# Moving the normalisation of token rows to GpSimd, and splitting a selection matrix, in a fused token, attention and expert kernel

## The reference, cut to what matters

```
# token layer: 8 steps along the sequence, up and down, width 64
a = einsum('bdl,od->blo', x, W1) + b1
for _ in range(8):
    up   = relu(a + shift_r(up) @ W2.T + b2)
    down = relu(a + shift_l(down) @ W2.T + b2)
h = relu(x*W3 + b3 + (shift_r(up) @ W4.T + b4) + (shift_l(down) @ W4.T + b4))
# attention layer, on the first norm of h: (h - mean) / sqrt(var + eps) over the 64 of a row
Q, K, V = norm(h) @ Wq.T, norm(h) @ Wk.T, norm(h) @ Wv.T
score[q, k, g] = relu(sum_d w_mlp[d] * relu(Q[q, g, d] - K[k, g, d]) + b_mlp)
h = h + softmax_k(score) @ V
# expert layer, on the second norm: 8 experts, the best 2 of each token
h = h + sum_e weight[e] * (gelu(norm(h) @ We1 + be1) @ We2 + be2)
```

## Time and profile before

| | us |
|---|---|
| median of 3 runs | 290.73 |
| the three runs | 289.77, 290.73, 297.43 |
| the profiled execution | 290.83 |
| its span in the trace | 288.6 |
| around the span | 2.23 |

### The profile page before, as it was taken

How to read it: one execution, slowest core, us unless ns; L and a number is a source line. 1 busy time by engine, 2 the same in 40 slices (tenths; PEclk the granted TensorE clock), 3 DMA queues, 4 the chain that set the end, 5 groups by cost and what they waited for, 6 DMA issues and landing times.

```text
span 288.6 us, 8043 instructions
## 1 busy us (share of the span) xinstructions
PE 267.2 (93%) x2954; PEld 97.8 (34%) x2954; DVE 243.2 (84%) x977; ACT 254.7 (88%) x646; POOL 41.3 (14%) x43
## 2 busy tenths in 40 slices
PE   8988999999999869899898999999988999999995
PEld 2444232333333223222233322333332223225463
DVE  2256999999999899999898999999989995783741
ACT  4345999999999999999999999999999999858462
POOL 3301100010000200104301110081110100041410
PEclk9999999999999999999999999999999999999999
DMA  6400000000000000050000000600000051002000
GB/s 157 143 0 2 5 2 2 0 3 2 2 1 2 1 2 2 1 141 10 0 2 1 2 2 9 159 2 0 2 1 3 2 134 34 1 0 76 8 16 20
DMA packets 5318, 6.90 MB, mean 24 GB/s; under 512 B 1632, under 2 KB 3272, under 8 KB 5280
## 3 DMA queue, kind: packets, MB, share of 16 engines
q1 hardware_dynamic: 5280, 6.40, 8.7%
HBM read 5.81 MB, written 0.58 MB: 22 GB/s over the span
## 4 chain that ended last, share of the span: by engine, by line
ACT 60%; PE 28%; DVE 7%; issue 3%; POOL 0%; DVEq 0%; ACTq 0%
ACT relu_ring L489 45%; PE bank L1203 7%; PE bank L946 6%; ACT hid L520 5%; PE bank L1083 5%; ACT sc_sb L498 4%; PE bank L988 3%; PE bank L952 3%; DVE relu_ring L640 1%; ACT state L458 1%; ACT L520 1%; PE bank L982 1%; ACT L498 1%; DVE sc_sb L655 1%; PE bank L1123 1%
## 5 line engine op out<-in xcount | busy, mean ns | idle before, releaser
L489 ACT ACTIVATE relu_ring<-bank,q_sb 128x256 f32<-128x256 f32 x421 | 163.1, 610 | 0.1
L640 DVE TENSOR_SCALAR relu_ring<-nk_sb,q_sb 128x256 f32<-128x256 f32 x568 | 155.5, 344 | 1.1 <-ACT nk_sb L474 1.0
L1083 PE MATMUL bank<-relu_ring,wsc 128*32 128x512 f32 x1024 | 127.1, 598 | 2.3 <-ACT relu_ring L489 1.1
L520 ACT ACTIVATE hid<-bank,b 128x512 f32<-128x512 f32 (+1 forms) x80 | 45.7, 644 | 9.8 <-PE bank L1203 9.7
L1083 PEld LDWEIGHTS bank<-relu_ring,wsc 128*32 128x32 f32 x1024 | 26.9, 109 | 57.5 <-issue 37.2
L1203 PE MATMUL bank<-xf,wf_sb 64*128 64x512 f32 (+1 forms) x160 | 40.4, 551 | 1.8 <-ACT hid L520 1.8
L946 PE MATMUL bank<-hid,wd 128*32 128x512 f32 (+1 forms) x320 | 31.6, 512 | 0.8 <-DVE prod L840 0.7
L393 POOL TENSOR_TENSOR rstd<-rstd,neg_half 128x4 f32<-128x4 f32 (+1 forms) x9 | 8.7, 966 | 108.1 <-DVE rstd L595 108.1
L1203 PEld LDWEIGHTS bank<-xf,wf_sb 64*128 64x128 f32 x160 | 14.6, 185 | 25.0 <-ACT hid L520 18.5
L840 DVE SCALAR_TENSOR_TENSOR prod<-bank,b,wbc 128x512 f32<-128x512 f32 (+1 forms) x20 | 12.8, 640 | 11.7 <-PE bank L946 8.5
L988 PE MATMUL bank<-state,tokw_sb 64*64 64x256 f32 x224 | 19.1, 407 | 2.9 <-DVE state L576 2.2
(11 more groups left out here) (104 smaller groups left out, 209.3 us busy)
## 6 DMA issues: line engine op xcount, KB each, us to landing
wbc<-gates SPq DMA_DIRECT2D x6, 512.0 KB, 5.8
wf_sb<-in_wf SPq DMA_DIRECT2D x1, 516.0 KB, 5.2
wd<-in_wd SPq DMA_DIRECT2D x1, 512.0 KB, 5.5
wbc<-gates SPq DMA_DIRECT2D x2, 256.0 KB, 4.1
out<-o_sb SPq DMA_DIRECT2D x3, 128.0 KB, 6.2
sel_f<-in_sel SPq DMA_DIRECT2D x1, 245.2 KB, 2.9
x_sb<-in_xw SPq DMA_DIRECT2D x1, 192.0 KB, 3.8
wa_sb<-in_wa SPq DMA_DIRECT2D x1, 192.0 KB, 3.4
```

The lines of the kernel that those rows point to most:

```text
L489: ins = nc.scalar.activation(relu_ring[:, n % RING, j, qi, :], keys, ACT.Relu, bias=q_sb[:, p, q:q + 1], scale=scale)
L520: nc.scalar.activation(hid[:, n % 8, 0:t], up_psum(k, i), ACT.Gelu, bias=b1[:, col:col + 1]).then_inc(gelu_ready, 1)
L640: ins = vec.tensor_scalar(relu_ring[:, n % RING, j, qi, :], nk_sb[:, p, :], q_sb[:, p, q:q + 1], 0.0, ALU.add, ALU.max)
L1083: ins = mm(bank[SCORE[blk % 2]][32 * j:32 * j + 32, :], wsc[:, s, :], relu_ring[:, n % RING, j].rearrange("p q k -> p (q k)"), start=(s == ...
```

## The change

DVE gives the normalised rows of the first norm of pairs 1 to 3, and of the second norm of units 0 to 2, to POOL: 24 tensor_scalar instructions, 12 of 128 x 64 and 12 of 128 x 128. POOL makes them right after its own power. DVE keeps pair 0's first norm and the second norms of units 3 and 4.

At the start, the selection matrix comes in two DMAs and is cast in two parts. The first three parts (which pair 0's inputs need) come first, on all 96 partitions; the last three are loaded and cast on 32 partitions only. PE stacks pair 0's inputs first and spreads the weights behind them; DVE instead of ACT casts them into `ws`. PE multiplies 7 blocks of zeros before, and 2 after, where there were 8 and 3. The two halves of `stack_inputs` have slots of their own.

All tables are new. `ACT_TILES` gives ACT 457 tiles instead of 456. Of the tables the diff below shows the two lines that the prediction speaks of.

```diff
     dict(
-        pe_stack=(-47,), pe_step=(-41, -39, -38, -36, -36, -35, -35, -34), pe_out=(-33,), pe_xa=(-24,),
+        pe_stack=(-44, -44), pe_step=(-42, -39, -38, -36, -36, -36, -33, -33), pe_out=(-31,), pe_xa=(-24,),
...
-WARM_UP, WARM_STACK, WARM_STEP, WARM_SLOTS = 8, 3, 1, 24
+WARM_UP, WARM_STACK, WARM_STEP, WARM_SLOTS = 7, 2, 1, 24
...
-        dve_top=(51,), dve_gates=(54,), dve_prod=(63, 66, 69, 71), dve_out=(78,), pool_norm=(55,),
-        pool_exp=(59,), pool_sum=(71, 71, 71, 74), dve_norm=(48,), dve_rec=(47,), dve_divide=(47,),
+        dve_neg=(36,), dve_pt=(38, 40, 41, 42), act_weigh=(46,), dve_resid=(47,), dve_xf=(50,),
+        dve_top=(51,), dve_gates=(55,), dve_prod=(63, 66, 69, 73), dve_out=(79,), pool_norm=(56,),
...
-            sp.dma_start(sel_f[:], sel_d).then_inc(ld_sel, 16)
+            sp.dma_start(sel_f[:, 0:3 * KX], sel_d[:, 0:3 * KX]).then_inc(ld_sel, 16)
+            sp.dma_start(sel_f[0:32, 3 * KX:], sel_d[0:32, 3 * KX:]).then_inc(ld_selw, 16)
...
             def norm1(p):
                 pool.wait_ge(h1_stats, p + 1)
                 inv_std(0).then_inc(rstd1_ready, 1)
+                if p >= 1:
+                    pool.wait_ge(rstd1_ready, p + 1)
+                    pool.wait_ge(xa_mm, p)
+                    for i in range(TT):
+                        ins = vec.tensor_scalar(xn1[:, i % 2, i // 2, :], h1[:, p, i, :], mv[:, 0, i, 0:1],
+                                                rstd[:, 0, i:i + 1], ALU.subtract, ALU.mult)
+                    ins.then_inc(xn1_ready, 1)
...
             def norm2(k):
                 pool.wait_ge(h2_stats, k + 1)
                 inv_std(1, UNITS[k]).then_inc(rstd2_ready, 1)
+                if k < len(UNITS) - 2:
+                    u = UNITS[k]
+                    pool.wait_ge(rstd2_ready, k + 1)
+                    if k >= 1:
+                        pool.wait_ge(xf_mm, k)
+                    for i in u.tiles:
+                        ins = vec.tensor_scalar(xn2[:, i], h2[:, u.pair % 2, i:i + 1, :].broadcast_to([P, 2, D]),
+                                                mv[:, 1, i, 0:1], rstd[:, 1, i:i + 1], ALU.subtract, ALU.mult)
+                    ins.then_inc(xn2_ready, 1)
...
             act.wait_ge(ld_sel, 16)
-            nc.scalar.copy(sel[:].rearrange("k s n -> k (s n)"), sel_f[:]).then_inc(sel_ready, 1)
-            act.wait_ge(ws_mm, 1)
-            nc.scalar.copy(ws[:, 0:D], bank[tokb(0)[1]][0:KX, 0:D]).then_inc(ws_ready, 1)
-            nc.scalar.copy(ws[0:64, D:2 * D], bank[tokb(0)[1]][0:64, D:2 * D]).then_inc(ws_ready, 1)
+            nc.scalar.copy(sel[:, 0:3, :].rearrange("k s n -> k (s n)"), sel_f[:, 0:3 * KX]).then_inc(sel_ready, 1)
+            act.wait_ge(ld_selw, 16)
+            nc.scalar.copy(sel[0:32, 3:6, :].rearrange("k s n -> k (s n)"),
+                           sel_f[0:32, 3 * KX:]).then_inc(sel_ready, 1)
...
+            dve.wait_ge(ws_mm, 1)
+            vec.tensor_copy(ws[:, 0:D], bank[tokb(0)[1]][0:KX, 0:D]).then_inc(ws_ready, 1)
+            vec.tensor_copy(ws[0:64, D:2 * D], bank[tokb(0)[1]][0:64, D:2 * D]).then_inc(ws_ready, 1)
...
+                if p == 0 and b == 1:
+                    pe.wait_ge(sel_ready, 2)
+                    for j in range(3):
+                        ins = mm(bank[tokb(0)[1]][0:KX, 0:WX], sel[0:KR, 3 + j, :], x_pc[0:KR, j, 0, 0:WX],
+                                 start=(j == 0), stop=(j == 2))
+                    ins.then_inc(ws_mm, 1)
                     keep_warm(WARM_STACK)
```

More of the change, by code:

```diff
@@ new lines @@
+    dict(
+        pe_stack=(-69, -65), pe_step=(-60, -58, -56, -55, -52, -50, -48, -45), pe_out=(-42,), pe_xa=(-34,),
+        pe_project=(-32,), act_stack=(-61,), act_step=(-60, -58, -57, -51, -50, -48, -45, -42),
+        act_out=(-41,), act_qk=(-24,), dve_step=(-60, -59, -58, -54, -53, -50, -47, -45), dve_stats=(-41,),
+        dve_xa=(-35,), dve_v=(-30,), pool_norm=(-44,), pe_values=(-31,), pe_keys=(2,), dve_mom=(-43,),
+        dve_aggr=(-43,)),
+    dict(
+        pe_stack=(-74, -74), pe_step=(-72, -70, -65, -64, -61, -57, -56, -54), act_stack=(-72,),
+        act_step=(-71, -66, -65, -63, -61, -58, -57, -55),
+        dve_step=(-72, -68, -66, -62, -61, -58, -56, -54), pe_out=(-52,), act_out=(-53,), dve_stats=(-52,),
+        pool_norm=(-59,), pe_xa=(-50,), dve_xa=(-49,), pe_project=(-47,), act_qk=(-48,), pe_values=(-46,),
+        dve_v=(-46,), pe_keys=(1,), dve_mom=(-52,), dve_aggr=(-52,))]
@@ L115 @@
[L115 removed]
+        dve_top=(50,), dve_gates=(50,), dve_prod=(58, 63, 65, 71), dve_out=(72,), pool_norm=(44,),
+        pool_exp=(45,), pool_sum=(47, 52, 59, 59), dve_rec=(45,), dve_divide=(45,), dve_mom=(45,),
+        dve_aggr=(45,), dve_stats=(45,), dve_lg=(49,), dve_gap=(50,), dve_num=(50,), dve_hot=(50,),
+        dve_den=(50,), dve_gw0=(50,), dve_gw1=(50,), dve_ohw=(50,)),
     dict(
[L117 removed]
@@ L962, in stack_inputs @@
                         pe.wait_ge(v_ready, FREED[p])
-                for b in range(2):
-                    if p >= 1 and b == 1:
-                        pe.wait_ge(xs_mm, 2 * p + 1)
-                    c = 1 + 2 * p + b
-                    rows = slice(32 * (c % 3), 32 * (c % 3) + KR)
-                    for i in range(3):
-                        ins = mm(stack_psum(p, b), sel[rows, i, :], x_pc[rows, i, c // 3, :],
-                                 start=(i == 0), stop=(i == 2))
-                    ins.then_inc(xs_mm, 1)
-                if p == 0:
+                else:
+                    pe.wait_ge(xs_mm, 2 * p + 1)
+                c = 1 + 2 * p + b
+                rows = slice(32 * (c % 3), 32 * (c % 3) + KR)
+                for i in range(3):
+                    ins = mm(stack_psum(p, b), sel[rows, i, :], x_pc[rows, i, c // 3, :],
+                             start=(i == 0), stop=(i == 2))
+                ins.then_inc(xs_mm, 1)
+                if p == 0 and b == 1:
[4 more added lines that the diff above has]
+                    ins.then_inc(ws_mm, 1)
                     keep_warm(WARM_STACK)
@@ L1246, in _ @@
             pe.wait_ge(sel_ready, 1)
-            pe.wait_ge(xpc0_ready, 1)
-            for j in range(3):
-                ins = mm(bank[tokb(0)[1]][0:KX, 0:WX], sel[0:KR, 3 + j, :], x_pc[0:KR, j, 0, 0:WX],
-                         start=(j == 0), stop=(j == 2))
-            ins.then_inc(ws_mm, 1)
             for n in range(FIRST, LAST):
@@ L1272, in _ @@
                 for p in range(PAIRS):
-                    for _ in due(n, p, TOKEN_AT[p], "pe_stack"):
-                        stack_inputs(p)
+                    for b in due(n, p, TOKEN_AT[p], "pe_stack"):
+                        stack_inputs(p, b)
                     for t in due(n, p, TOKEN_AT[p], "pe_step"):
```

116 lines of the change are left out of this document (50 added, 66 removed), and 8 rows, old and new, of the table ACT_TILES.

## The result

| | before | changed |
|---|---|---|
| median of 4 runs each, us | 290.55 | 294.07 |
| all runs, us | 289.77, 290.36, 290.73, 297.43 | 293.84, 294.07, 294.08, 294.5 |
| the profiled execution, us | 290.83 | 293.84 |
| its span, us | 288.6 | 292.1 |

The ratio of the changed kernel to the one before is 1.0132, with an interval of [1.0107, 1.0158]: slower by some 3.8 us. The ratio goes by the undisturbed runs, so the 297.43 us before is left out of it. The forecast was 291.3 us, with a range of 287.5 to 295.5, and "within 2%" as the likeliest class. Both held. The sum was 2.5 us too low against the profiled execution, and this chapter is about where those came from.

What follows compares the result with a forecast made beforehand. The prediction took the kernel as a 27.6 us start, then ACT's list, then a full PE stretch. +2.4 - 0.7 - 0.7 + 0 - 0.5 = +0.5 us on 290.83 gave 291.3 us, range 287.5 to 295.5.

Steps and rivals of the forecast that it cites:

- the 33rd gelu: Sign at unit 2's first gelu, 225.7 us before: to come 0.5 to 1.5 us later.
- Bound: From first tile to unit 2's gelus, ACT's list sets the time: busy 197.79 of 198.10 us.
- ACT's list, +2.4: Up to unit 2's first gelu: four more tiles, 1.6 us, and pair 1's two `last` instructions, 0.8 us.
- Relief of DVE, -0.7: In the slots, less DVE work lets ACT lose two hidden waits: -0.7 us, bounds 0 and -3.
- DVE sets the pace as well: Rival, chance 0.10: DVE's lists decide the slots, so 6.6 us come off them, giving 283.0 us.
- The start, -0.7: Before the first tile: keys 1.3 us earlier, less waits of 0.5 and 0.1 us for pair 1's steps.
- The handover, 0: POOL's normalised rows to PE: 0.3 us a tile, lateness covered; pair 3 and unit 1 bounds 0 and +3 us.
- The end, -0.5: Last PE stretch: PE's 0.52 us wait for unit 3's gates goes, with two score copies ahead instead of four.
- GpSimd is starved: Rival, chance 0.11: DVE's tiles hold up POOL's rows, 4.4 us late at unit 1, 3 at pair 3; 298.7 us.
- The lock works both ways: Rival, chance 0.15: POOL's rows make DVE's tiles wait, about 7 us laid on DVE, relief nil; 292.0 us.

Runs made afterwards that it cites:

- eight_tiles_less: Changed kernel with one ACT tile left out in each of eight slots, made by nobody: 293.0 us, ratio 1.0059.
- rows_shared: Kernel before with the new start, first norms of pairs 1 to 3 on GpSimd, second norms of units 0 to 2 split two and two with DVE: 289.77 us, 0.9975.
- rows_on_dve: Changed kernel with all 24 rows' instructions back on DVE, new start and new tables kept: 296.15 us, ratio 1.0172.
- new_start_rows_on_pool: Kernel before with the new start and the 24 rows on GpSimd, every other step at its old place: 294.95 us, ratio 1.0135.
- new_start_first_on_pool: Kernel before with the new start and only the first norms of pairs 1 to 3 on GpSimd, old tables: 289.07 us, ratio 0.9939.
- the zeros: Changed kernel with 12 blocks of zeros multiplied by PE in its wait before pair 3's turning: 293.95 us, ratio 1.0069.
- the two kernels that were to tell it: Changed kernel with ACT_TILES as before (304.82 us, 1.0469), and changed kernel with UNIT_AT and KEEP_AT as before (301.1 us, 1.0344).

## Why the prediction was right, and where it was wrong

The class and the range were right. The profiled execution took 293.84 us, where the sum gave 291.3. The slots' stretch grew by 4.7 us where the steps gave +2.4 and -0.7: 3.0 too low (1.6 of it is ACT's new idle time, 0.7 the relief that didn't come, 0.7 busy time beyond the count). The end's -0.5 didn't come. Against that the first tile came 1.2 us earlier where the start was to gain 0.7, and the part around the span, which the sum took as unchanged, shrank by 0.5. That is 3.0 + 0.5 - 0.5 - 0.5 = 2.5 us. So luck has a share in how near the number came: 1.0 us of errors the other way. Of the signs named beforehand one was plainly missed: the 33rd gelu was to come 0.5 to 1.5 us later and came 3.5 us later (229.20 against 225.7). By its own steps:

**Bound.** Right for the kernel before: the slots run at ACT's list. With the new start and the old tables they are again 198.08 us, with ACT busy for 197.77.

**ACT's list, +2.4.** By count right, and ACT's busy time in the slots grew by 3.1 us. The other 0.7 isn't traced to a place. That the whole list lies on the path was too strong: `eight_tiles_less` gave back part only.

**Relief of DVE, -0.7.** It didn't come. With the first norms alone off DVE, where PE waits 0.46 us at most for GpSimd, the ratio is 0.9939 against 0.9937: twelve instructions taken off DVE are worth nothing, within 0.4%. This fits the first reading of the profile, that DVE's load is not what the slots run at. *DVE sets the pace as well* (283.0) is out.

**The start, -0.7.** -1.2 at the first tile, between two executions that both took 1.07 us for their first `state` multiplies, and ACT then waits 0.16 us for pair 1's `last`: -1.0. The projection began at 24.32 us instead of 25.78, 1.5 us earlier where I had 1.3, and the `state` between keys and tiles took 0.3 us, without the wait that I had put before it. In the tables of before the same code is worth 2.0 us at the first tile and 1.8 by the ratio, with the quicker first multiplies in it.

**The handover, 0: the step that failed.** "I take 0.3 us, four in 1.2 us against DVE's 1.1", and "at pair 3 and unit 1 I take no loss, with bounds 0 and +3". By their medians a row tile of 128 x 64 takes GpSimd 0.59 us and one of 128 x 128 0.91. That is over twice and three times what a tile took on DVE (four in 0.97 and in 1.11 us), and my 0.3 leaned on a copy of 512 columns in 0.61 us, which didn't scale down to the small tiles. The second norms are 2.3 us later. In the tables of before units 1 and 2 have no cover for that, and it costs 5.7 us. With the new start and the old tables, unit 2's eps step ended at 213.3 us and PE began to turn the rows at 215.8: 2.5 us, in which the power (1.05) and DVE's rows (1.1) just fit, and GpSimd's 3.4 don't.

```profile
213.16 0.17 DVE L596 TENSOR_SCALAR rstd<-mv 128x4 f32<-128x4 f32 x1
214.64 1.10 DVE L742 TENSOR_SCALAR xn<-h,mv,rstd 128x128 f32<-128x128 f32 x4
```

```profile
215.81 0.66 PE L1158 MATMUL bank<-ident,xn 128*128 128x128 f32 x4
```

I had called unit 2 covered by counting slots in the new tables, which turn it one slot later (50 for 49), and there it held, barely: GpSimd delivered at 222.56 us, and PE turned the rows at 222.62 without a wait. At the two places where I took no loss there was one. At pair 3 PE waited 3.22 us and ACT then 0.72; at unit 1 PE waited 1.54 us and ACT 0.43. So the new tables absorb most of unit 2's loss and a part of unit 1's. What they pay for it, by the trace, is ACT's longer list and pair 3, where PE turns one slot earlier and falls to the lower clock. Rows with new tables (1.0132) end where rows with old tables (1.0135) do, each 2.0% behind the new start alone: as a whole the tables win nothing back.

**The end, -0.5.** It didn't come: 62.15 us against 62.1. PE's wait for unit 3's gates went (it turns them at 262.43 us without idle time before), and the stretch is none the shorter for it.

**The rivals.** *GpSimd is starved* (298.7, chance 0.11) had the right engine, unit 1 as a place and the wrong mechanism. It wanted four row tiles of over 5 us, held up by DVE; those of the second norms took 3.4 to 3.7, most of it GpSimd's own time. The shortest, at unit 1 while DVE stood idle, took 0.79 us against the median of 0.91: being held up is some 0.12 us a tile by that estimate. Single tiles took longer: one of 128 x 64 took 1.14 us in the changed kernel against 0.57 for the shortest, and the 1.29 us of `rows_shared` stand against 0.79. *The lock works both ways* (292.0, 0.15): in the groups of DVE's tiles the 24 rows on GpSimd add 0.9 us (568 tiles, 155.6 us with the rows on DVE and 156.5 without); measurable, and a seventh of the 6.2 us given away. The Trainium skill, "SBUF — State Buffer", section "SBUF: two separate sides", has the second engine block fully; the trace agrees for the copy of 5.13 us, and shows for the rows at most these 0.5 to 0.6 us a tile.

**My first theory after the result**, that GpSimd's rows make the wait at pair 3, fell as the whole cause with `rows_on_dve`. What stands: the second norms on GpSimd cost 5.7 us in the places of before, lower clock included (shown by `new_start_rows_on_pool` against `new_start_first_on_pool`), the lower clock behind pair 3's wait costs 0.86 us up to the 33rd gelu of the changed kernel (shown by the zeros), and the start gains 1.8 us by the ratio. How the rest of the new tables' cost splits between ACT's four tiles, its `last` instructions and hidden waits stays open: the two kernels that were to tell it broke the tables.

**The better version.** The new start in the kernel before, with all rows on DVE or with only the first norms on GpSimd, beats both kernels: 0.9937 [0.9911, 0.9963] and 0.9939 [0.9904, 0.9973].
